# Attention block on one core: the two query buffers moved by 64 bytes, nothing else changed

## The reference, cut to what matters

```python
xn = layernorm(x)                       # x: (1, 2048, 256)
qkv = einsum('bsd,ed->bse', xn, Wqkv)   # 16 heads, D = 128, for q, k and v
logits = einsum('bqhd,bkhd->bhqk', q, k) * D ** -0.5
w = softmax(logits)                     # 2048 x 2048 for each head
out = einsum('bhqk,bkhd->bqhd', w, v)
y = x + out.reshape(S, H * D) @ Wout.T + ffn(xn)
# ffn: three ternary weights (704 wide), sigmoid(x1) * x2, then back to 256
```

## Time and profile before

| | before |
|---|---|
| median of 3 runs | 1899.84 us (1899.81 to 1901.06) |
| the profiled execution: time | 1899.86 us |
| its span, first to last instruction | 1898.0 us |
| TensorE busy | 1855.2 us, 98% of the span |
| weight loads busy | 1659.1 us, 87% |
| VectorE, GpSimd, ScalarE busy | 84%, 72%, 66% |
| mean granted TensorE clock | 0.996 of full speed |

### The profile page before, as it was taken

The page is one execution under the profiler, slowest core; times in us unless marked ns, Lnnn a source line. Parts: engine busy times, 40 slices in busy tenths (PEclk is TensorE's granted clock), DMA queues, the critical chain, the costliest instruction groups (busy, mean ns, idle before and its releaser), DMA issues.

```text
span 1898.0 us, 33380 instructions
## 1 busy us (share of the span) xinstructions
PE 1855.2 (98%) x11556; PEld 1659.1 (87%) x11556; DVE 1599.3 (84%) x2098; ACT 1254.7 (66%) x1702; POOL 1358.2 (72%) x515
## 2 busy tenths in 40 slices
PE   5979999999999999999999999999999999999998
PEld 4869888898989889898888989888898988899887
DVE  7478888888888888888888889888898988888895
ACT  4456666776667677666767666676766667676664
POOL 4438677876868787686877768687776868776675
PEclk9999999999999999999999999999999999999999
DMA  3037667676767767676776767677676767767664
GB/s 125 1 92 170 162 160 180 156 170 161 168 162 163 182 152 173 159 167 162 166 179 153 171 159 169 161 170 176 154 170 160 167 162 172 174 153 171 158 160 127
DMA packets 195912, 298.73 MB, mean 157 GB/s; under 512 B 37905, under 2 KB 57105, under 8 KB 195857
## 3 DMA queue, kind: packets, MB, share of 16 engines
q1 hardware_dynamic: 195856, 298.08, 67.1%
HBM read 12.71 MB, written 2.10 MB: 8 GB/s over the span
## 4 chain that ended last, share of the span: by engine, by line
PE 79%; POOL 6%; SPq 5%; issue 4%; DVE 3%; DMA 1%; ACT 1%; POOLq 0%; DVEq 0%; ACTq 0%
PE ps_o L398 31%; PE ps_s L389 10%; PE ps_s L390 10%; PE ps_s L391 10%; SPq L306 4%; POOL parts L1120 4%; PE ps_t L379 4%; PE ps_t L369 4%; PE ps_s L360 3%; PE ps_s L435 2%; PE ps_o L407 1%; PE ps_o L409 1%; PE ps_o L408 1%; DVE prob L969 1%; DMA raw<-prob 1%
## 5 line engine op out<-in xcount | busy, mean ns | idle before, releaser
L1120 POOL TENSOR_TENSOR parts<-raw,parts 128x2048 fp32r<-128x2048 f32 x254 | 1175.3, 4628 | 441.7 <-ACT parts L732 441.3
L744 ACT ACTIVATE prob<-ps_s,neg_max 128x1024 f32<-128x1024 f32 x512 | 567.0, 1114 | 448.6 <-DVE neg_max L963 448.6
L959 DVE TENSOR_REDUCE row_max<-ps_s 128x1 f32<-128x1024 f32 x512 | 613.1, 1213 | 113.4 <-PE ps_s L391 95.2
L969 DVE STREAM_TRANSPOSE prob<-prob 128x1024 f32<-128x1024 f32 x508 | 599.5, 1218 | 58.4 <-ACT prob L744 58.0
L732 ACT CAST parts<-raw 128x2048 fp32r<-128x2048 f32 x254 | 486.4, 1915 | 102.8 <-DMA raw<-prob 102.6
L398 PE MATMUL ps_o<-parts,v_hi 128*128 128x256 f32 x4064 | 515.6, 280 | 2.8 <-POOL v_lo L1113 2.8
L398 PEld LDWEIGHTS ps_o<-parts,v_hi 128*128 128x128 f32 x4064 | 497.9, 189 | 18.4 <-POOL v_lo L1113 5.9
L389 PE MATMUL ps_s<-k_hi,q_hi 128*128 128x512 f32 x1024 | 403.2, 394 | 11.2 <-ACT prob L744 10.3
L390 PE MATMUL ps_s<-k_lo,q_hi 128*128 128x512 f32 x1024 | 401.0, 392 | 0.0
L391 PE MATMUL ps_s<-k_hi,q_lo 128*128 128x512 f32 x1024 | 400.6, 391 | 0.0
L398 PE MATMUL ps_o<-parts,v_lo 128*128 128x256 f32 x2032 | 275.7, 278 | 0.0
(11 more groups left out here) (115 smaller groups left out, 1564.7 us busy)
## 6 DMA issues: line engine op xcount, KB each, us to landing
raw<-prob SPq DMA_DIRECT2D x2032, 128.0 KB, 2.4
v_raw<-v_turned SPq DMA_DIRECT2D x244, 64.0 KB, 2.0
w_raw<-wqkv_dram SPq DMA_DIRECT2D x32, 128.0 KB, 2.6
y<-x_dram SPq DMA_DIRECT2D x4, 512.0 KB, 4.8
wo_raw<-wqkv_dram SPq DMA_DIRECT2D x16, 128.0 KB, 2.5
wo_raw<-wo_dram SPq DMA_DIRECT2D x16, 128.0 KB, 2.3
out_dram<-y SPq DMA_DIRECT2D x8, 256.0 KB, 2.7
w_raw<-w_dram SPq DMA_DIRECT2D x2, 704.0 KB, 7.6
```

Source lines behind the costliest of these rows:

```text
L744: nc.scalar.activation(tile, logit, ACT.Exp, bias=neg_max[:, t:t + 1], scale=SCALE, accum_out=row_sum[:, t, half:half + 1]).then_inc(s_exp, 1)
L959: nc.vector.reduce_max(row_max[:, t, half:half + 1], ps_s[:, 2 * half:2 * half + 2, :].rearrange("p b n -> p (b n)"), AX_X).then_inc(s_mx, 1)
L969: nc.vector.transpose(tile, tile).then_inc(s_xp, 1)
L1120: nc.gpsimd.tensor_tensor(half_of(0, half), moved(p, half), half_of(1, half), ALU.subtract).then_inc(s_pl, 1)
```

## The change

Two buffers of 64 bytes in each partition are declared at another place. `neg_max` comes to stand ahead of `q_hi`, which moves `q_hi` and `q_lo` up by 64 bytes. `denom` comes to stand behind `q_lo`, so that the buffers from `xn` and `v_hi` to `row_max` move up by 128 bytes, which leaves them as they were modulo 128. `row_sum` moves up by 64 bytes. Everything from `inv_denom` on (`prob`, `raw`, `parts`, the buffers of the feed-forward network) stays where it was, and so does everything up to `k_lo`. On each engine the instructions, their order and their waits are the same.

```diff
         k_hi = sb("k_hi", [P, S], F32R)
         k_lo = sb("k_lo", [P, S], F32R)
+
+        neg_max = sb("neg_max", [P, T])
         q_hi = sb("q_hi", [P, 2, 512], F32R)
         q_lo = sb("q_lo", [P, 2, 512], F32R)
+        denom = sb("denom", [P, T])
...
         row_max = sb("row_max", [P, T, 2])
-        neg_max = sb("neg_max", [P, T])
         row_sum = sb("row_sum", [P, T, 2])
-        denom = sb("denom", [P, T])
         inv_denom = sb("inv_denom", [P, T])
```

## The result

The changed kernel takes 1925.54 us (median of 4 runs, 1924.27 to 1926.03), the kernel before, on the same chips, 1900.14 us. The ratio is 1.0132, 95% interval 1.012 to 1.0145: 25 us slower. The range of the prediction ended at 1917.

The account below looks back on a forecast made before the run. The prediction took TensorE to bound the kernel. Logits +10.1, half products -8.0, projections +1.8 and output projection +0.7 sum to +4.6 us on 1899.86, so 1904.5 us, with a range from 1887 to 1917.

Parts of the forecast that it names:

- slower, 0.47: Whole kernel: the change makes it slower, chance 0.47, against 0.33 for the same time and 0.20 for faster.
- What bounds the kernel: Steady part, 300 to 1800 us: TensorE waits for nobody, so each matmul's nanosecond counts one to one; other engines have 13% room.
- The buffers that move by 128 bytes keep their place modulo 128 ... costed at nothing.: Products, projections and transfers on the buffers moved by 128 bytes: no change, cost nothing.
- The logits, +10.1 us: 3072 logits matmuls of 512 columns: slow to 231 ns as in ffn_up, 3.3 ns each, +10.1 us (bounds +3.7 and +16.3).
- The half products behind the logits, -8.0 us: 111 half products directly behind disturbed logits: 2.73 us instead of 2.82, four fifths counted, -8.0 us (bounds nothing and -10.0).
- Products behind the output projection, 0: Half products behind the output projection: stay at 2.73 us as before, no cost.
- Projections, +1.8: Six projections behind a half product that became quick: 1.38 us instead of 1.36, 109 times, +1.8 us (bounds 0 and 2.2).
- Output projection, +0.7: First matmul of each output projection, behind disturbed logits: 120 ns instead of 114, 125 times, +0.7 us.
- The small buffers, nothing: neg_max, denom and row_sum: accessed 16 or 32 numbers at a time by engines with room, cost nothing.
- the logits suffer and the products stay: Rival: logits slow down, products behind them stay at 118 ns; +10.8 us, 1910.6 us, up to 1917; chance 0.22.
- The all-quick case: Rival: logits at 226.7 ns and products behind them at 114; -13.1 us, 1886.8 us; chance 0.17.
- That nothing happens: Rival: addresses have no effect on the matmuls, time stays at 1899.8 us; chance 0.13.

Follow-up runs that it names:

- e1: Kernel before with keys and queries both 64 bytes further, and v, w_sp, o and wo 128 bytes further: 1916.43 us, ratio 1.0085.
- e4: Kernel before with keys 64 bytes further and queries, v, w_sp, o and wo 128 bytes further: 1925.26 us, ratio 1.0131.
- e8: Kernel before with keys and queries unchanged and what lies behind them 128 bytes further: 1914.76 us, ratio 1.0073.
- e9: Kernel before with queries 64 bytes further and what lies behind them 256 bytes further: 1912.76 us, ratio 1.0066.
- e7: Kernel before with o_hi and o_lo, the output projection's weights, 64 bytes further: 1901.11 us beside 1901.26, ratio 1.0.
- e10: Kernel before with keys and queries unchanged and what lies behind them 256 bytes further: 1901.2 us, ratio 1.0.
- e12: Kernel before with queries 192 bytes further and what lies behind them 256 bytes further: 1900.71 us beside 1901.51, ratio 0.9999.
- e11: Kernel before, addresses kept, each output projection split over two steps, three matmuls ahead of every half product: 1898.67 us beside 1901.51, ratio 0.9983.
- the map: Separate kernel without the computation: series of matmuls on weight tiles in 32-byte steps from the moving operand; 512 columns took 226.7 to 234.3 ns each.
- the kernel of series: Separate kernel of matmuls alone: 12 of 512 columns, k of 256, then 24 of 256 at distance 64; the 24 took 2.99 or 2.88 us.

## Why the prediction was wrong

The sign was right (slower, 0.47), the size was not: +4.6 us forecast, +25 measured. By its steps:

- *What bounds the kernel.* TensorE is the bound in the steady part, as it said, but "one nanosecond more or less for each matmul goes into the time one to one" was too simple. The pace alone cost 33.3 us, and the span grew by 24.5, since TensorE then waited less: the excess of the long distances is 31 to 33 us in every kernel that is slower than the one before (e1 to e4, e8, e9) and about 40 in those at its speed (e7, e10, e12). The other way round, a quicker one waits more, for GpSimd (e11). That VectorE's 13% of room leave TensorE the bound says nothing of such waits.
- *"The buffers that move by 128 bytes keep their place modulo 128 ... costed at nothing."* This is the step that failed first. The period is 256 bytes (e10 and the map), and the 128 bytes alone cost 14 us (e8): in that kernel's trace +10.1 us in the products and +6.9 in the projections, less 2.8 in the output projection, where waits fell away. The prediction named the projections as the place where this would show, and there it shows. But it took the period from the words of the change and asked no row for it.
- *The logits, +10.1 us.* The mechanism was right, the term mis-sized: 5.1 ns each instead of 3.3, +15.7 us by pace and +14.5 with the waits, inside the upper bound of +16.3. `ffn_up` was the wrong model, since its distance modulo 256 is 192 and not 64. Its 233 ns in one stretch and 229 in another are two paces of the same distance, 192 (228.8 in the map). What stands ahead doesn't sort them: three groups of `ffn_up` follow the same 44 matmuls of `ffn_down`, and in the kernel before one of them holds 233 and two come down to 229 within five matmuls, while in the changed kernel all three hold 233. Why is open. That the wrong model's upper bound, 233, is what the logits came to is luck.
- *The half products behind the logits, -8.0 us.* Nothing, for two reasons. In the changed kernel no product is quick any more, at distance 192. And logits at distance 64 don't hand over the quick pace: with `v` kept 64 from `parts` only 8 of 111 got it (e9), against 7 before. At distance 192 they do, 100 of 111 (e12), and there this term comes out near its forecast, -7.1 us for all products by distances. The logits then cost +4.2, not +10.1.
- *Products behind the output projection, 0.* 114.3 to 117.9 ns, +3.6 ns x 24 x 126 = +10.9 us by pace in the changed kernel; with the queries unmoved (e8) they are at 117.8 as well, so it is the 128 bytes.
- *Projections, +1.8.* +5.1, and for another reason: the 128 bytes (e8), and not a quick product ahead.
- *Output projection, +0.7.* -3.9. Its pace stayed (118.8 and 118.7 ns); long distances at it fell from 31 to 6.
- *The small buffers, nothing.* Nothing, as e7 and e10 show, which put them elsewhere at the old time. They are used one or two numbers per partition at a time, not 16 or 32 as the prediction has it.
- *The rivals.* That the logits suffer and the products stay describes e9, 1912.8 us against its 1910.6, and not the changed kernel, whose other products slowed down. The all-quick case is excluded: at 64, 128 and 192 the logits' mean was 229.2 ns or more. That nothing happens is excluded too. By the Trainium skill's rule of independent read ports (TensorE: Matmul & The Clock Gate, "Step-by-step: what each phase is for"), loading weights takes nothing from the running matmul, and the distance should not matter. In the map it costs up to 7.6 ns per matmul of 512 columns and 6.7 of 256, 3% and 6%, so the rule doesn't hold to the last per cents. Whether the loss arises at the reads is not shown.

Why the best distance is 0 for 512 columns and 64 for 256 stays open, and so does what exactly passes from one kind of matmul to the next.

## What to carry to other kernels

Where TensorE is the bound and weights are loaded for every matmul (no run here did without), look at the distance between matmul starts, not at busy time, and compare it for the same instruction at different places. Tabulate the start of weights minus the start of the moving operand modulo 256 bytes: a small buffer that is declared elsewhere shifts everything behind it, and here 64 or 128 bytes were worth 12 and 14 us of 1900. A gain in pace is worth its full sum only as long as no other engine is waited for: in e11 10.5 us in the products became 2.8 in the time. Before a price is taken from a similar stretch, check that the two are alike in what the change is about, to a wider modulus than the change names.

## What was not expected of the hardware

- The pace of matmuls with a weight load each depends on the distance of the two buffers modulo 256 bytes: 226.7 to 234.3 ns for 512 columns, 113.3 to 120.0 for 256. The best distances differ (0 and 64).
- The same 24 matmuls settle at 113.3 or 117.8 ns, by what ran before them, without any other engine at work (the kernel of series).
- Distances of 226.7 and 113.3 ns are 544 and 272 cycles of 2.4 GHz at a granted clock of 1.00, 17 for each 16 columns, at the best of all distances. In the kernel before, `ffn_up` matmuls of 512 columns start 427 ns apart from 40.32 to 43.30 us, where the granted clock is 0.50, the level of 1.2 GHz: that is 512 cycles, one for each column, at the same distance of 192 that costs 229 to 233 ns at the full clock.
